# TensorE transposes weight row i-1 instead of row i at each place of the weight preparation

## The reference

```python
# cross attention, 16 heads of 32, over 77 context rows
x = x + xattn(layernorm(x), ctx, ctx, mask, Wq, bq, Wk, bk, Wv, bv, Wo, bo)
# FFN with fp4 quantisation; all three weights are quantised too
def fp4_linear(x, w):               # blocks of 16 along the last dim:
    return einsum('bsk,nk->bsn', fp4_quant_dequant(x), fp4_quant_dequant(w))
z = layernorm(x)
h = silu(fp4_linear(z, w_gate)) * fp4_linear(z, w_up)     # 512 -> 1408
x = x + fp4_linear(h, w_down)                             # 1408 -> 512
```

## Time and profile before

| | |
|---|---|
| median of 3 runs | 2112.87 us (2111.06 to 2114.29) |
| the profiled execution | 2118.97 us, span 2116.8 us |
| TensorE products busy | 1964.8 us, 93% of the span |
| VectorE, ScalarE, GpSimd busy | 1750.4 (83%), 1211.4 (57%), 477.9 (23%) us |
| transposes of gate and up (L594) | 88, the first at 76.2 us, the last at 200.0 us |

### The profile page before, as it was taken

One profiled execution on the slowest core, in us unless ns is written; L12 is line 12 of the kernel. 1 busy time (PEld: TensorE's weight loads), 2 busy tenths in 40 slices (PEclk: granted clock), 3 DMA queues, 4 the chain that ended last, 5 costly groups with the idle time before them and its releaser, 6 DMA issues.

```text
span 2116.8 us, 63066 instructions
## 1 busy us (share of the span) xinstructions
PE 1964.8 (93%) x24960; PEld 1225.6 (58%) x24960; DVE 1750.4 (83%) x2676; ACT 1211.4 (57%) x2489; POOL 477.9 (23%) x525
## 2 busy tenths in 40 slices
PE   6334899999999999999999999999999999999987
PEld 4222566666666656666666666666666666666653
DVE  7776688888888888888888888888888888888873
ACT  4443566566665666556665556665566655666521
POOL 4453112112221122212222122221222212122110
PEclk9655999999999999999999999999999999999998
DMA  4232455554556555555555554555555555555541
GB/s 167 75 80 66 81 116 120 137 126 113 119 120 142 127 117 116 120 136 127 118 116 127 134 129 116 115 123 132 131 121 116 123 130 132 116 116 124 122 93 53
DMA packets 660741, 248.18 MB, mean 117 GB/s; under 512 B 612598, under 2 KB 613622, under 8 KB 660702
## 3 DMA queue, kind: packets, MB, share of 16 engines
q1 hardware_dynamic: 659118, 247.66, 50.8%
q10 hardware_dynamic: 1584, 0.01, 0.0%
HBM read 65.97 MB, written 34.82 MB: 48 GB/s over the span
## 4 chain that ended last, share of the span: by engine, by line
PE 88%; issue 4%; POOL 4%; DMA 2%; DVE 1%; ACT 1%; SPq 0%; POOLq 0%; another core or an unknown queue 0%; ACTq 0%
PE psum L609 43%; PE psum L538 38%; PE psum L631 4%; POOL h_room L477 2%; PE psum L659 2%; POOL h_room L481 1%; DMA t_room<-halves 1%; PE psum L618 1%; DMA ph_room<-h_room 0%; DMA q_room<-in_L_xattn_Wk_dram 0%; ACT probs L774 0%; SPq L353 0%; PE psum L551 0%; PE psum L594 0%; DVE h_room L860 0%
## 5 line engine op out<-in xcount | busy, mean ns | idle before, releaser
L609 PE MATMUL psum<-wguT,t_room 128*128 128x352 bf16 x6144 | 942.4, 314 | 14.7 <-DVE h_room L1048 7.6
L609 PEld LDWEIGHTS psum<-wguT,t_room 128*128 128x128 bf16 x6144 | 600.0, 98 | 336.7 <-DVE h_room L1048 8.5
L538 PE MATMUL psum<-wdT,ph_room 128*128 128x512 bf16 x2112 | 472.1, 382 | 11.4 <-DMA ph_room<-h_room 11.4
L502 POOL TENSOR_TENSOR ln_var_eps<-ln_mean_var,eps 128x1 f32<-128x1 f32 x128 | 100.7, 787 | 1419.5 <-DVE ln_mean_var L1018 1037.2
L768 ACT ACTIVATE silu_g<-psum 128x352 f32<-128x352 f32 x256 | 118.6, 463 | 525.6 <-PE psum L609 525.5
L538 PEld LDWEIGHTS psum<-wdT,ph_room 128*128 128x128 bf16 x2112 | 207.8, 98 | 265.4 <-DMA ph_room<-h_room 12.3
L774 ACT ACTIVATE probs<-psum,neg_max 128x77 f32<-128x77 f32 x1024 | 243.7, 347 | 25.7 <-DVE neg_max L1054 25.0
L538 PE MATMUL psum<-t_room,wqT 128*128 128x128 bf16 x3072 | 200.0, 223 | 3.6 <-DMA t_room<-halves 2.4
L538 PEld LDWEIGHTS psum<-t_room,wqT 128*128 128x128 bf16 x3072 | 179.0, 100 | 17.8 <-DMA t_room<-halves 2.8
L538 PE MATMUL psum<-woT,t_room 128*128 128x512 bf16 x768 | 179.0, 383 | 0.4 <-DMA t_room<-halves 0.4
L1054 DVE TENSOR_REDUCE neg_max<-psum 128x8 f32<-128x616 f32 x128 | 101.8, 796 | 91.1 <-PE psum L659 91.1
(11 more groups left out here) (103 smaller groups left out, 2506.0 us busy)
## 6 DMA issues: line engine op xcount, KB each, us to landing
io_room<-in_x_dram SPq DMA_DIRECT2D x128, 256.0 KB, 3.0
x_scratch<-x_new SPq DMA_DIRECT2D x64, 256.0 KB, 2.6
x_cur<-x_scratch SPq DMA_DIRECT2D x64, 256.0 KB, 2.7
out_dram<-io_room SPq DMA_DIRECT2D x64, 256.0 KB
t_room<-halves SPq DMA_TRANSPOSE x192, 3.2
raw<-in_L_ffn_w_down_dram SPq DMA_DIRECT2D x4, 704.0 KB, 4.1
raw<-in_L_ffn_w_gate_dram SPq DMA_DIRECT2D x11, 256.0 KB, 2.6
raw<-in_L_ffn_w_up_dram SPq DMA_DIRECT2D x11, 256.0 KB, 2.9
```

The costliest lines, as they stand in the source:

```text
L538: ins = pe.matmul(dst, left(i), right(j), start=first and n == 0, stop=last and n == len(PRODUCTS) - 1)
L609: ins = pe.matmul(ps[:, 0:CW], xqT[:, i, kc, :], wguT[:, which, j, kc, cols], start=(kc == 0 and i == j), stop=(kc == KC - 1 and i == LO))
```

## The change

TensorE's `gate_up(i)` transposes row i-1 instead of row i. The call for row 0 ahead of the steps is gone (place 1 does it), and row 10, which no place has now, is transposed in `weights_end`. The other engines' code is as it was.

```diff
-            def gate_up(i):
+            def gate_up_transposes(i):
                 for half in range(2):
                     pe.wait_ge(w_quant, 2 * i + 2 * KC + half + 1)
                     at_least(pe, w_lo, 2 * i + half - 1)
...
+            def gate_up(i):
+                gate_up_transposes(i - 1)
+
             def weights_end():
+                gate_up_transposes(IC - 1)
                 pe.wait_ge(w_lo, 2 * IC)
-
-            gate_up(0)
```

## The result

| | before | changed |
|---|---|---|
| median, fastest to slowest | 2113.58 us (2111.06 to 2115.97, 4 runs) | 2099.78 us (2097.66 to 2101.23, 4 runs) |
| ratio, 95% interval | | 0.9934 [0.9917, 0.9951] |
| profiled execution | 2118.97 us, span 2116.8 | 2099.75 us, span 2097.6 |

The change makes the kernel 13.8 us faster by the medians; the interval gives 10 to 18 us. A second measurement of it, e11, gave 2099.21 us against 2113.74, ratio 0.9934 [0.9922, 0.9946].

The account below looks back on a forecast made before the run. The weight stretch, 76 to 202 us, was taken as bound by VectorE, idle where attention blocks stood behind waiting transposes. Gains 2.7 + 8.6 = 11.3 us, taken from 2112.87, gave 2101.6; range 2098.3 to 2106.3.

Parts of the forecast that it names:

- q(0) and scores(0): Tile 0's query projection and score products: projection starts at the same time, scores start at 100.0 for 100.89, gain 0.9 us.
- the fast end: Lower-time bound: transposes behind tile 0's query projection at full clock (1.3 early), quicker landing and projection for tile 1; sum 12.9 us.
- pv(0): Tile 0's products with the values: run at about 125 to 126.4, before VectorE is ready, so its 4.87 us wait goes.
- q(1): Tile 1's query projection: holds row 5's transposes and copy, a new VectorE wait of about 5 us giving most back.
- scores(1): Tile 1's score products: wait only for the queries' low part, start 144.1 for 146.81; gain 2.7 us, including the early 0.9.
- o(0): Tile 0's output projection: runs 147.3 to 152.2, ahead of row 7's transposes, so VectorE's 8.60 us residual wait goes whole.
- From there on: From tile 0's residual (164.26) to the start of tile 0: VectorE sets every step, so all moves as one piece.
- (b): Rival: tile 0's output projection is late and VectorE waits again, giving half back; at 5 us late 2107; chance 0.08.
- (c): Rival: no change, 2113, since the queue already looks past the wait or something unmoved holds tile 0's start; chance 0.05.
- the rule on the queue: Skill page's rule that TensorE may pull weight loads ahead; if whole blocks passed waiting transposes, the sum would be 0.
- (d): Rival: slower, as tile 0 could begin and stay at the lower clock, +25 - 11.3, so 2127; chance 0.05.
- 2 us to either side: Allowance for the clock in tiles 0 and 1: a third of at most 6 us, should it fall out otherwise.

Follow-up runs that it names:

- e11: The changed kernel, unchanged, run again for a second profile and a comparison on one chip: 2099.21 us against 2113.74, ratio 0.9934.
- e8: The kernel before, unchanged, run again for a second profile and a null comparison: 2112.83 us, ratio 1.0002.
- e5: The kernel before with only the values products of tile 0 and the query projection of tile 1 moved ahead of row 5's transposes: 2112.11 us, ratio 0.9995.
- e7: The changed kernel with rows 1 and 5 transposed ahead of the query projections, plus 18 unread 512-column products around row 10's transposes: 2101.71 us, ratio to before 0.9955.
- e10: The changed kernel with rows 1 and 5 transposed ahead of the query projections and score banks cleared at the projections' start: 2090.65 us, ratio to before 0.9895.
- e1: The kernel before with only the output projection of tile 0 moved ahead of row 7's transposes: 2105.58 us against 2112.44, ratio 0.9964.
- e2: The changed kernel with the output projection of tile 0 put back behind row 7's transposes: 2110.42 us, ratio to before 0.9987.

## Why the prediction was right

Forecast 2101.6 us, -11.3; measured 2099.78, -13.8 against the median beside it. D puts the weight stretch at -12.2. Against the medians of before measured beside the experiments (2112.44, 2112.48, 2113.74) the changed kernel's two medians stand 12.7 to 14.5 lower, so what is beyond 12.2 is 0.5 to 2.3 us, about what two medians of the same kernel differ by (2112.44 and 2113.74). It is not shown that the change gains anything outside the weight stretch. The profiled executions differ by 19.2: 12.1 to tile 0, 4.6 in tiles 0 to 2 and 2.5 behind. e8 has 77.66 us in place of 81.28 and 2.4 us less behind, so nearly all of the last two belongs to that execution (the traced executions of e5 and e7 have the same longer part behind).

- *q(0) and scores(0)*, 0.9 forecast: T(1) behind the projection ran at the upper clock (granted clock 1.00 from 93 us), eight transposes in 1.04 us where I had 1.1 for half of them. The copy came at 93.55, not 93.9, and scores(0) at 99.73, 1.2 earlier. It is the fast end that the bounds had named. (Before, this copy did not stand at 92.13 because of T(1), whose first half was over at 85: it stood behind the mask. e10 shows what that was worth.)
- *pv(0)*, forecast 125 to 126.4: 124.64 to 126.0, and VectorE's wait is gone.
- *q(1)*, "where most of that is given back": right, and e5 shows it alone. The input landed 3.1 us behind its issue (127.72 to 130.81), not 3.7, and the projection stayed wholly at the lower clock, 5.8 us and not 5.2. These two misses were 0.6 us each and cancelled, which is luck; with the first half of T(5) again short, the copy of row 5 came at 137.25 instead of 138.0. The new wait of "about 5 us" is 4.44.
- *scores(1)*, gain 2.7: it is 3.4 (143.43 for 146.81), the 0.7 from the line above. This is the term that was mis-sized.
- *o(0)*, gain 8.6: VectorE goes to the residual without a wait at 152.18. e1 and e2 give 8.7 and 8.5. The projection itself was over at 149.33 and not at 152.2: its 11 products on record took 2.82 us, since the clock was at its upper level (granted clock 0.99 from 147 to 150 us).
- *From there on* everything moved as one piece: the residual 12.08 earlier, the values products of tile 1 12.12.
- *The rivals.* (b), o(0) late, didn't occur; the margin was 2.9 us where 0.8 was forecast, most of that from the clock. (c) and the rule on the queue: no product passed a waiting transpose, in before or in e2. (d): tile 0 did not stay low (granted clock 1.00 from 195 to 205 us). The two profiles of before differ by 3.6 us in the stretch of tiles 0 to 2, about the width named as 2 us to either side. In the longer one the clock rose later in tile 0 (granted clock 0.50 from 205 to 210 us, 0.73 in e8), and in tile 1 the query projection waited 2.38 us for its input and then ran in part at the lower level (0.50 from 236 to 238 us). That the clock alone made the difference is not shown.
- *The sums.* By its own terms the slow end of q(0) and scores(0) is 0.3 and not 0.1 (0.9 less 0.64), and the upper end of the range is 2106.0 and not 2106.3. Neither matters for the measured time.

## What to carry to other kernels

When an in-order engine serves two streams, look at what stands directly behind each long wait, not at the sum of the wait: here 91 us of waiting on TensorE was worth 12, and one block behind one wait (8.6 us on VectorE) was most of that. Taking the work one place late everywhere was right at three places and wrong at two; where a consumer on another engine waits for the late work in its own order (ScalarE's copies in front of the grid steps), put it ahead of the block whose input isn't there yet anyway. Then follow that consumer's order one step further back: its mask, waiting for a clearing in the middle of a block, was worth 5.5 us more.

## What the runs showed that was not expected

18 more products on TensorE (and as many weight loads) just ahead of tile 0 brought a stop of 1.96 to 2.04 us on TensorE, for which the profile shows no cause, in all three kernels that had them, whether they were 512 or 128 columns long. It stands behind the first product of the query projection each time.

The traces hold a lead. In several kernels without the added products the same projection has a short stop, behind its 19th product: 0.47 us in before, 0.26 in e11 and e10, 0.28 in e1, 0.23 in e5.

```profile
193.71 0.69 PE L538 MATMUL psum<-t_room,wqT 128*128 128x128 bf16 x5 [0.26 <-issue]
```

So with 18 products added the stop comes 18 products earlier: counted in TensorE's instructions it stands at the same point of the program. And the part on the DMA queues shows a read of the queue named "instruction" there, 0.8 to 1.2 us behind the start of the values products of tile 1 in every kernel looked at. This is e7 from 180 to 190 us; of its two reads the first starts at 186.1, and TensorE goes on at 188.72:

```profile
q8 instruction: 2, 0.03, 1.4%
```

In all kernels with a stop TensorE goes on 2.6 to 2.9 us behind the start of this read. A wait for the next piece of the program fits this: with the added products TensorE comes to that point 2 us sooner behind the read. No run tested it.
